# One-core attention and mixture-of-experts kernel on Trainium2: small VectorE instructions rewritten as tensor_reduce, the top-8 strike placed behind the split of h1, and the router's high and low weights stacked as one 32-column operand

## What is computed

```python
mod = (_silu(L0_c) @ L0_wmod).reshape(32, 6, 1, -1)   # sa, ca, ga, sb, cb, gb
h = _layernorm(x) * (1 + ca) + sa
x = x + ga * attention(h)        # q, k, v are Givens rotations of h, softmax, then
                                 # ave / sqrt(|sum(ave*ave*sgn)|)
h = _layernorm(x) * (1 + cb) + sb
x = x + gb * ffn(h)

def ffn(h):                      # E = 16 experts, cap = 64 rows of each batch to each expert
    logits = einsum('bsd,ed->bse', h, gate_w)
    scores = softmax(logits).transpose(0, 2, 1)
    topk_w, topk_idx = top_k(scores, cap)
    x_tok = take_along_axis(h, topk_idx)
    eo = einsum(gelu(x_tok @ Wg) * (x_tok @ Wu), Wd) * topk_w
    out = zeros.at[flat_idx].add(eo)
    return out + shared          # shared: the same gated network on all rows
```

## Time and profile before

| | us |
|---|---|
| median of 3 runs | 2397.8 |
| lowest and highest of them | 2396.78, 2400.62 |
| profiled execution | 2398.3 |
| its span, first to last instruction | 2396.5 |
| TensorE busy | 2288.7 |
| VectorE busy | 1558.3 |
| GpSimd busy | 1483.4 |
| ScalarE busy | 1091.5 |

### The profile page before, as it was taken

One profiled execution on the slowest core, in us unless ns is written; L12 is line 12 of the kernel. 1 busy time (PEld: TensorE's weight loads), 2 busy tenths in 40 slices (PEclk: granted clock), 3 DMA queues, 4 the chain that ended last, 5 costly groups with the idle time before them and its releaser, 6 DMA issues.

```text
span 2396.5 us, 40463 instructions
## 1 busy us (share of the span) xinstructions
PE 2288.7 (96%) x13620; PEld 1989.4 (83%) x13620; DVE 1558.3 (65%) x3098; ACT 1091.5 (46%) x2107; POOL 1483.4 (62%) x1253
## 2 busy tenths in 40 slices
PE   5999999999989999998989999999999999999997
PEld 4788888888878888787878888888888888888886
DVE  6777777887877888788766555455555554555543
ACT  4555665555645555564543333333333333333332
POOL 3566676666655666656555666666666666666664
PEclk8999999999999999999999999999999999999999
DMA  2212212211212121121243434444434444443433
GB/s 94 67 54 70 74 62 70 71 57 62 75 54 67 53 70 57 62 75 53 71 122 72 89 58 86 86 87 91 83 61 87 85 88 85 87 87 59 87 62 44
DMA packets 83002, 175.19 MB, mean 73 GB/s; under 512 B 12272, under 2 KB 47248, under 8 KB 82864
## 3 DMA queue, kind: packets, MB, share of 16 engines
q0 software_dynamic: 49152, 67.14, 17.5%
q1 hardware_dynamic: 33712, 106.05, 13.1%
HBM read 105.84 MB, written 67.31 MB: 72 GB/s over the span
## 4 chain that ended last, share of the span: by engine, by line
PE 69%; DVE 16%; issue 7%; ACT 4%; POOL 3%; DMA 0%; DVEq 0%; SPq 0%; ACTq 0%; POOLq 0%
PE ps L372 22%; PE ps L373 21%; PE ps L374 21%; PE ps L531 2%; DVE hidden_f L928 2%; DVE bn_stats L811 2%; ACT stage L668 1%; DVE neg_max L968 1%; DVE stage L912 1%; DVE stage L915 1%; DVE x_t L806 1%; ACT gelu L684 1%; DVE score_rows L1023 1%; PE ps L447 1%; POOL rstd L1204 1%
## 5 line engine op out<-in xcount | busy, mean ns | idle before, releaser
L372 PE MATMUL ps<-x_t,weights 128*128 128x512 f32 x1536 | 613.2, 399 | 41.8 <-DVE hidden_f L928 32.2
L1318 POOL DMA_INDIRECT out<-x_rows,step_token x256 | 417.9, 1632 | 308.9 <-DVE x_rows L1148 250.1
L373 PE MATMUL ps<-x_t,weights 128*128 128x512 f32 x1536 | 601.3, 391 | 0.0
L374 PE MATMUL ps<-x_t,weights 128*128 128x512 f32 x1536 | 599.6, 390 | 0.0
L372 PE MATMUL ps<-weights,hidden 128*128 128x256 f32 x2048 | 587.6, 287 | 10.0 <-POOL hidden L1208 4.9
L374 PE MATMUL ps<-weights,hidden 128*128 128x256 f32 x2048 | 581.6, 284 | 0.0
L373 PE MATMUL ps<-weights,hidden 128*128 128x256 f32 x2048 | 581.5, 284 | 0.0
L1171 DVE TENSOR_TENSOR hidden_f<-gelu,ps 128x512 f32<-128x512 f32 x256 | 175.6, 686 | 379.3 <-ACT gelu L786 325.4
L372 PEld LDWEIGHTS ps<-weights,hidden 128*128 128x128 f32 x2048 | 394.3, 193 | 19.3 <-issue 8.3
L373 PEld LDWEIGHTS ps<-weights,hidden 128*128 128x128 f32 x2048 | 394.5, 193 | 6.1
L786 ACT ACTIVATE gelu<-ps 128x512 f32<-128x512 f32 x256 | 152.4, 595 | 539.1 <-PE ps L374 522.8
(11 more groups left out here) (175 smaller groups left out, 3603.1 us busy)
## 6 DMA issues: line engine op xcount, KB each, us to landing
pairs<-mod_rows SPq DMA_DIRECT2D x36, 512.0 KB, 4.4
x_rows<-in_x SPq DMA_DIRECT2D x32, 512.0 KB, 3.5
h_rows<-stage SPq DMA_DIRECT2D x32, 512.0 KB, 2.6
out<-y_rows SPq DMA_DIRECT2D x32, 512.0 KB, 2.9
stage<-in_wg SPq DMA_DIRECT2D x16, 512.0 KB, 3.7
stage<-in_wd SPq DMA_DIRECT2D x16, 512.0 KB, 4.9
stage<-in_wu SPq DMA_DIRECT2D x16, 512.0 KB
mod_rows<-mod_rows SPq DMA_DIRECT2D x31, 256.0 KB, 3.2
```

The source lines that it names most:

```text
L372: pe.matmul(o, lhs(HI), rhs(HI), start=start, stop=False)
L373: pe.matmul(o, lhs(HI), rhs(LO), start=False, stop=False)
L374: return pe.matmul(o, lhs(LO), rhs(HI), start=False, stop=stop)
L1318: pool.indirect_dma_start(out=out_rows, out_offset=bass.IndirectOffsetOnAxis(ap=ICUR[g][:, t:t + 1], axis=0), in_=X1[:, g % 2, t * D:(t + ...
```

## The change

Nine edits, in the order of the file:

1. The router's weights lie as [k, part, expert] and are used as one operand of 32 columns (16 high, 16 low) against the high rows, and as 16 columns (high) against the low rows: four matmuls a batch and not six. The logits come out as two halves that must be added. Their copy (GLT) and transposes are 32 rows high.
2. `gate_max` adds the halves with a tensor_reduce from PSUM into a new SBUF tile GLS, takes the maximum from GLS, and subtracts it from GLS. Both inputs of the subtraction are then in SBUF; before, one was in PSUM. The wait of `a_times_v` on `gl_ready` is not changed.
3. The exp bias (L973), a tensor_scalar, becomes a tensor_reduce over three numbers: the negated maximum and two constants, written once in setup.
4. The maximum in out_norm (L934), a tensor_tensor of two SBUF tiles, becomes a tensor_reduce over a tile of pairs.
5. The copy of a group's scores (L1003) becomes a tensor_reduce over one element.
6. The top indices (L1028), a tensor_scalar that adds the row of the batch's first token, become a tensor_reduce over one element; the first token is added in `top_slots` instead, once a group.
7. The strike of the first round goes from before hidden(i-1, 1) to behind h1_low, except where a group starts (iterations 10, 18 and 26).
8. GpSimd writes the tile FIRST with 32 memsets at the start.
9. ZZ and SSQ are two columns of one tile.

The diff, cut to its core:

```diff
@@ gate(n), TensorE
-                    mm = mm3(PD[0:E, 512:512 + S], lambda a: GW[:, a, k, :], lambda a: H2_T[:, a, k, :],
-                             k == 0, k == KD - 1)
+                    pe.matmul(PD[0:2 * E, 512:512 + S], GW[:, k, :, :].rearrange("p a e -> p (a e)"),
+                              H2_T[:, HI, k, :], start=k == 0, stop=False)
+                    mm = pe.matmul(PD[0:E, 512:512 + S], GW[:, k, HI, :], H2_T[:, LO, k, :],
+                                   start=False, stop=k == KD - 1)
@@ score_max, VectorE (NM is now [P, T, 3]; columns 1 and 2 hold constants)
-                dve.tensor_scalar(NB[:, both], NM[:, both], SCB[:, 5:6], SCB[:, 4:5], ALU.add,
-                                  ALU.add).then_inc(ebias, 2)
+                dve.tensor_reduce(NB[:, both], NM[:, both, :], AX.X, ALU.add).then_inc(ebias, 2)
@@ out_norm
-                dve.tensor_tensor(NSQ[:, :], ZZ[:, :], SSQ[:, :], ALU.max).then_inc(norm_sq, 1)
+                dve.tensor_reduce(NSQ[:, :], SQ_ZZ[:, :, :], AX.X, ALU.max).then_inc(norm_sq, 1)
@@ gate_max
-                logits = PD[:, 512:512 + T * E].rearrange("p (t e) -> p t e", t=T)
-                dve.tensor_reduce(GMX[:, :], logits, AX.X, ALU.max).then_inc(gmax_ready, 1)
+                dve.tensor_reduce(GLS[:, :, :], PD[:, 512:512 + T * 2 * E].rearrange("p (t a e) -> p t e a", t=T, a=2),
+                                  AX.X, ALU.add).then_inc(gls_ready, 1)
+                dve.wait_ge(gls_ready, n + 1)
+                dve.tensor_reduce(GMX[:, :], GLS[:, :, :], AX.X, ALU.max).then_inc(gmax_ready, 1)
                 dve.wait_ge(gmax_ready, n + 1)
-                dve.tensor_tensor(GL[:, :, :], logits, GMX[:, :].unsqueeze(2).to_broadcast((P, T, E)),
+                dve.tensor_tensor(GL[:, :, :], GLS[:, :, :], GMX[:, :].unsqueeze(2).to_broadcast((P, T, E)),
                                   ALU.subtract).then_inc(gl_ready, 1)
@@ group_scores
-                dve.tensor_copy(ROW[1][:, :].rearrange("p (t n) -> p t n", t=T),
-                                SG[...]).then_inc(group_set, 1)
+                dve.tensor_reduce(ROW[1][:, :].rearrange("p (t n) -> p t n", t=T),
+                                  SG[...].unsqueeze(3), AX.X, ALU.max).then_inc(group_set, 1)
@@ top_strike
-                dve.tensor_scalar(TOPI[:, :, bass.ds(r * 8, 8)], BESTU[:, :].unsqueeze(1).to_broadcast((P, 2, 8)),
-                                  CONST[:, bass.ds(g + C_BASE, 1)], None, ALU.add).then_inc(top_kept, 1)
+                dve.tensor_reduce(TOPI[:, :, bass.ds(r * 8, 8)],
+                                  BESTU[:, :].unsqueeze(1).to_broadcast((P, 2, 8)).unsqueeze(3), AX.X,
+                                  ALU.max).then_inc(top_kept, 1)
@@ iteration, VectorE
                     top_best(odd)
-                    top_strike(odd, g, r, before)
+                    if start is not None:
+                        top_strike(odd, g, r, before)
                 if start is not None:
                     group_scores(start)
                 if valid(i - 1):
                     hidden(i - 1, 1)
                 if valid(i + 1):
                     h1_low(i + 1)
+                for g, r, before in rounds[:1]:
+                    if start is None:
+                        top_strike(odd, g, r, before)
```

More of the change, by code:

```diff
@@ L129, in block_kernel @@
         GMX = sb("gate_max", [P, T])
-        GLT = sb("gate_logits_t", [E, S])
+        GLT = sb("gate_logits_t", [2 * E, S])
+        GLS = sb("gate_logits_sum", [P, T, E])
         GL = sb("gate_logits", [P, T, E])
@@ L748, in iteration @@
                     wait(act, gate_t_done, i - 1)
-                    act.copy(GLT[:, :], PD[0:E, 512:512 + S]).then_inc(gate_read, 1)
+                    act.copy(GLT[:, :], PD[0:2 * E, 512:512 + S]).then_inc(gate_read, 1)
                     gelu(i - 1, 0)
@@ L967, in score_max @@
                     dve.wait_ge(s_done, n * T + t + 1)
-                    dve.tensor_reduce(NM[:, t:t + 1], PC[:, t * S:(t + 1) * S], AX.X, ALU.max,
+                    dve.tensor_reduce(NM[:, t:t + 1, 0], PC[:, t * S:(t + 1) * S], AX.X, ALU.max,
                                       negate=True).then_inc(nmax, 1)
@@ L1035, in top_slots @@
                     rows = slice(h * CAP, (h + 1) * CAP)
-                    for o, dst in ((0, IDX), (P, WGT)):
-                        last = dve.tensor_copy(
-                            dst[rows, :, bass.ds(g * TT, TT)],
-                            ps[rows, o:o + P].rearrange("p (q h e) -> p h e q", h=2, e=E)[:, h])
+                    slots = (ps[rows, o:o + P].rearrange("p (q h e) -> p h e q", h=2, e=E)[:, h] for o in (0, P))
+                    dve.tensor_tensor(IDX[rows, :, bass.ds(g * TT, TT)], next(slots),
+                                      FIRST[rows, bass.ds(g * TT, TT)].unsqueeze(1).to_broadcast((CAP, E, TT)), ALU.add)
+                    last = dve.tensor_copy(WGT[rows, :, bass.ds(g * TT, TT)], next(slots))
                 last.then_inc(tops_read, 1)
@@ L1193, in _ @@
         def _(pool):
+            for q in range(NG * TT):
+                for h in range(2):
+                    last = pool.memset(FIRST[h * CAP:(h + 1) * CAP, q:q + 1], float((2 * q + h) * S))
+            last.then_inc(first_set, 1)
+            pool.wait_ge(first_set, 1)
             pool.wait_ge(consts_in, 16)
@@ L1228, in exp_sum_squares @@
                 wait_apart(pool, norm_sq, n)
-                pool.tensor_tensor(ZZ[:, :], Z[:, :], Z[:, :], ALU.mult).then_inc(zz_squared, 1)
+                pool.tensor_tensor(ZZ, Z[:, :], Z[:, :], ALU.mult).then_inc(zz_squared, 1)
                 wait_apart(pool, zz_squared, n + 1)
-                pool.tensor_scalar(ZZ[:, :], ZZ[:, :], 1e-8, None, ALU.mult).then_inc(zz_ready, 1)
+                pool.tensor_scalar(ZZ, ZZ, 1e-8, None, ALU.mult).then_inc(zz_ready, 1)
             def v_low(n):
```

32 lines of the change are left out of this document (18 added, 14 removed).

## The result

| | before | after |
|---|---|---|
| median, us | 2398.4 (2395.2 to 2401.2, 20 runs) | 2405.6 (2398.6 to 2410.6, 20 runs) |
| ratio | | 1.0027, 95% interval 1.0019 to 1.0035 |
| profiled execution, us (span) | 2398.3 (2396.5) | 2410.6 (2408.8) |

The account below looks back on a forecast made before the run. Two bounds within 0.3 us: TensorE's own work and the way over VectorE, GpSimd and ScalarE. Terms sum to +8.4 on 2398.3, 2406.7; the median 0.5 lower, 2406.2, stated as 2406.5, range 2399 to 2418.

Parts of the forecast that it names:

- The subtraction waits, and for one operation only: In gate_max, the two-SBUF-input subtraction waits for GpSimd's L1217 (v_swap_part), ending 2.6 us after ln1_modulate's end on VectorE (E).
- Rival A: In gate_max, the subtraction does not wait beside L1217: together -45 us, 2353, faster; chance 0.09.
- rival B: In gate_max, the subtraction waits for both GpSimd operations, L1217 and L1223: +66 us, 2472; chance 0.06.
- TensorE's restart: At a_times_v(i, 1), TensorE starts at E (ln1_modulate's end) + 2.68; next K (its keys' start) at E + 8.48.
- The two saved matmuls: Router's product on TensorE: 0.46 us less a batch, worth 0 in iterations 1 to 30, -0.9 at the end.
- Exp bias: L973 takes 0.16, but L951 then waits for GpSimd's L1245 by itself, so K to E shrinks by only 0.2.
- K to E: From the keys' start on TensorE (K) to ln1_modulate's end on VectorE (E): 28.32 us, forecast to become 28.1.
- Rival C: After the exp bias, L951 does not wait for GpSimd: -10 us, 2397, no change; chance 0.08.
- The strike: First round's strike, moved behind h1_low, ends near E (ln1_modulate's end) + 8.1, before hidden(2) is due: cost 0.
- the missing cover: The strike's 1.2 us of slack, there only through TensorE's new wait; without it the move would cost up to 0.7.
- The group copies: Score copies as reduces take about 0.66 us: +0.7 in iteration 10, +0.3 each in 18 and 26 with other changes.
- few us: Left open in the bounds: two further stalls where an engine waits at a loop's edge could move by this much.

Follow-up runs that it names:

- e9: The changed kernel with GpSimd's v_swap_part made as two operations of 128x512 instead of one of 128x1024; 2371.4 us.
- e5: The changed kernel with gate_max(i-1) moved on VectorE from behind ln1_modulate(i+1) to before it; 2349.0 us.
- e2: The kernel before with only the router's changes: stacked weights, four matmuls, sum of halves, subtraction from SBUF; 2441.3 us.
- e4: The kernel before, six router matmuls kept, with logits put into SBUF by a one-element reduce and both subtraction inputs read there; 2441.1 us.
- e8: The kernel before with only the exp bias made a tensor_reduce over three numbers; 2394.3 us.
- e6: The changed kernel with the first round's strike back in its old place before hidden(i-1, 1); 2412.1 us.
- e1: The changed kernel with TensorE's attention product waiting for the sum of the halves (gls_ready), not for the subtraction (gl_ready); 2383.6 us.
- e3: The changed kernel without the router's changes: six matmuls and the subtraction from PSUM as before, all other edits kept; 2360.3 us.
- e7: The kernel before with only top_indices as a one-element reduce, the first token added once a group from the tile GpSimd writes; 2368.0 us.

## Why the prediction was right, and where it was off

The forecast of 2406.5 met 2405.6, and the steps that carried it were each seen.

- *The subtraction waits, and for one operation only.* Forecast: 2.0 long, ending at E + 2.6. Measured: 2.08, ending at E + 2.57. Rival A (0.22) and rival B (4.4) fall by the timeline above, and e9 shows that the wait follows the length of that operation: half the operation, half the time (1.00). That v_own_part starts behind it without keeping it out was argued from the copy in the earlier trace rows and held. The rule of the Trainium skill (SBUF — State Buffer, Who interferes with whom) that the prediction weighed, by which a VectorE instruction with two inputs in SBUF contends with a GpSimd instruction that reads SBUF, agrees: 2.08 beside v_swap_part, 0.22 in e5 beside an idle GpSimd.
- *TensorE's restart.* Forecast E + 2.68 and next K at E + 8.48; measured E + 2.71 and E + 8.40. Periods forecast 36.6 and 36.7, measured 36.6 and 36.7.
- *The two saved matmuls are worth 0* in the changed kernel: e2 against e4.
- *Two readings of the rows* were slightly off, without changing a term. L1028 does not end inside L1223 but 0.03 behind its end (518.24 against 518.21), in keeping with the wait that the prediction gave it. And L951 starts inside L1245 in 30 cases, not 31.
- *Exp bias.* K to E forecast 28.1, measured 341.62 - 313.51 = 28.11 in iteration 8 (K = 313.51). Rival C falls: L957 waits for v_sum by itself, and e8 gains 6 us with the start's share among them, not 10 or more beside it. Iteration 0 was forecast at -1.6 and gave -1.5 (29.58 to 28.07). Its K0, priced at nothing with the setup, came 0.8 later; over the twelve profiles K0 lies between 25.0 and 27.3, with no order by edits, so the 0.8 cannot be put down to the change.
- *The strike* was priced at 0. With the changed kernel's late K that holds, and its new place even saves 0.26 a round (e6). What I wrote of the missing cover, "up to 0.7", was too low: e1 shows 1.0, since I took hidden(2) for the next to be late and overlooked the chain norm_squares, out_factor, attention_out.
- *The sum by its terms.* Iterations 2 to 9 were forecast at +12.1 and gave 293.03 - 280.98 = +12.05. Iteration 1 gave +0.3 and not +1.0. The group copies, forecast at +0.7, +0.3 and +0.3, gave +0.7 in iteration 10 (37.07 for 36.40) and +0.5 in 26 (39.65 for 39.17). Each copy took 0.67 to 0.69 for a forecast of 0.66; the old form had taken 2.49 once, beside v_swap_part, and 0.41 to 0.42 in the three other places, so only the first became shorter. In iteration 18 the stall at a loop's edge went from 7.39 to 5.60, and the whole from 44.68 to 43.26. Iteration 19, the first behind it, became shorter by 1.2 more. These 2.7 are of the size of the "few us" that the prediction had left open; why they moved was not tested.
- *What was missing* is TensorE's clock (last section). Three iterations between K20 and K27 (21, 23 and 25) took 38.3 to 38.5, where the kernel before took 36.9 to 37.0, +4.4 together, in a stage forecast at -0.3. Iteration 27, too, ran partly at the lower clock and gave +1.4 for a forecast of -0.1, the other three with two rounds -1.8 for -2.1. The profiled execution of the changed kernel was the slowest of its 20. At the median the clock's share is smaller, and the loop's edge works against it, so that the forecast came within 1 us is in part luck: in the profile the largest error of a stage is 4.4 us, and the sum is off by 3.9 (+12.3 for +8.4).

What the prediction did not say, because it followed the wait as written: the change held a gain of 39 us (e3), most of it (33 us) in one 16-element instruction (e7), and lost it to one 64-element instruction in a bad place.

## What to carry to other kernels

Before moving an operand from PSUM to SBUF, look at what GpSimd runs at that moment: an instruction of 64 elements took 2.08 us beside a GpSimd operation and 0.22 us a few instructions earlier, with the same waits. Look for the place where both VectorE and GpSimd stand idle and put small two-input instructions there; where none is, wait on the last read of the shared buffer and not on the last result. And when an instruction's wait for GpSimd goes, check whether the next one has two SBUF inputs: the wait may only move, as from the exp bias to ln2_centre.

## What the runs showed of the hardware

TensorE's granted clock fell after some of the new waits. Two neighbouring iterations of the changed kernel, and inside the second the 3.4 us behind the wait for the subtraction (PEclk, the third number from the end, is 1.00, 0.96 and 0.52):

```profile
761.81:798.32 36.51, 34.93 (x216) 30.18 (x214) 29.36 (x66) 21.05 (x44) 23.82 (x20) 1.00 0.19 66
798.32:836.66 38.34, 36.47 (x216) 31.67 (x214) 29.90 (x66) 20.90 (x44) 24.72 (x21) 0.96 0.18 62
...
829.40:832.80 3.40, 3.33 (x16) 3.37 (x17) 2.23 (x4) 1.59 (x3) 3.40 (x2) 0.52 0.01 5
```

In the second, 256-column matmuls start every 0.213 us and not every 0.12, so the engine works at 1.2 GHz and not at 2.4, after it had stood 0.41 and then 1.41 us. Such an iteration costs 1.5 to 1.6 us more: iteration 13 of the same kernel, which stood 0.37 and 1.41 us at the same two places and kept its clock, takes 36.78, and iteration 23, which stood 0.37 and 1.41 as well and lost it, 38.29. Between K2 and K31, and the loop's edge in iteration 18 left aside, where every profile shows half clock, the profiled execution has three such stretches of 3.4 us behind the wait for the subtraction, all between K20 and K27, and one at K27, behind the stall of 2 us for score_rows that a new group brings. That of the kernel before, where TensorE stood 1.3 to 1.5 us in each iteration with one round at another place, has none in either stage. e2 has five of them, e4 none, though both wait as long: in e2 an iteration without a round takes 38.31 at a clock of 0.96, in e4 36.84 at 1.00.

```profile
206.55:244.86 38.31, 36.46 (x216) 31.65 (x214) 27.85 (x59) 20.88 (x44) 23.55 (x20) 0.96 0.18 62
```

```profile
207.56:244.40 36.84, 35.38 (x217) 30.37 (x216) 27.85 (x59) 21.03 (x44) 23.62 (x20) 1.00 0.19 64
```

So such a wait does not always lower the clock, and its length alone does not decide it. That fits the spread of the 20 times of the changed kernel, 12 us against 6 before: the six under 2402 us have a mean clock of 0.990 to 0.992, the seven above 2408 one of 0.987 to 0.989. The idle times cost more than their own length, in some executions and not in others, and I could not say which of them will. What decides it was not tested.
